# Latents' cross attention: context normalised with features over partitions, running maxima put into the score banks by ScalarE

## The reference

```python
def layernorm(t, g, b):
    mu = jnp.mean(t, axis=-1, keepdims=True)
    var = jnp.var(t, axis=-1, keepdims=True)
    return (t - mu) * jax.lax.rsqrt(var + EPS) * g + b
xn = layernorm(x, ln_x_g, ln_x_b)              # x: the context, 512 features
ln = layernorm(latents, ln_l_g, ln_l_b)
q = ln @ Wq                                    # 16 heads of 64
k, v = jnp.split(jnp.concatenate((xn, ln), axis=1) @ Wkv, 2, axis=-1)
sim = jnp.einsum('bhid,bhjd->bhij', q * scale, k)
sim = jnp.where(mask_full[:, None, None, :], sim, max_neg)
out = jnp.einsum('bhij,bhjd->bhid', softmax(sim), v)
return layernorm(out.transpose(0, 2, 1, 3).reshape(b, m, INNER) @ Wout, ln_o_g, ln_o_b)
```

## Time and profile before

| what | value |
|---|---|
| median of 3 runs | 2112.92 us (2111.11 to 2114.09) |
| the profiled execution's own time | 2115.48 us |
| its span, first to last instruction | 2113.3 us |
| mean granted clock of PE | 0.970 |
| busy: PE, DVE, ACT, POOL | 94%, 74%, 49%, 31% of the span |
| the pipeline of `context_attention_1` | about 820 to 1852 us |
| span of one body in it | 59.5 us |

### The profile page before, as it was taken

The page is one execution under the profiler, slowest core; times in us unless marked ns, Lnnn a source line. Parts: engine busy times, 40 slices in busy tenths (PEclk is TensorE's granted clock), DMA queues, the critical chain, the costliest instruction groups (busy, mean ns, idle before and its releaser), DMA issues. The chain is left out here.

```text
span 2113.3 us, 45029 instructions
## 1 busy us (share of the span) xinstructions
PE 1977.3 (94%) x18290; PEld 1103.7 (52%) x18290; DVE 1569.6 (74%) x2777; ACT 1044.0 (49%) x1484; POOL 657.6 (31%) x696
## 2 busy tenths in 40 slices
PE   7899999999789788999999999999999999888998
PEld 3455555555555443455555555555555555544643
DVE  4689999999857673677777777777777776654676
ACT  2689998998813542333333333333333333323453
POOL 3244444454412230133333322333333322313100
PEclk9899999999799899999999999999999999999999
DMA  4323323322133210000000000000000000210300
GB/s 149 103 54 99 93 65 95 97 64 72 31 142 116 108 41 22 22 23 23 23 4 20 23 23 23 23 23 23 23 2 23 23 23 2 81 46 0 145 21 20
DMA packets 39613, 106.22 MB, mean 50 GB/s; under 512 B 19312, under 2 KB 21616, under 8 KB 33264
## 3 DMA queue, kind: packets, MB, share of 16 engines
q1 hardware_dynamic: 39408, 103.35, 16.1%
HBM read 75.42 MB, written 1.05 MB: 36 GB/s over the span
## 5 line engine op out<-in xcount | busy, mean ns | idle before, releaser
L1468 POOL TENSOR_SCALAR a1c_p_hi<-a1c_pf 128x512 f16<-128x512 f32 x272 | 201.1, 740 | 666.6 <-ACT a1c_pf L1524 624.1
L1326 PE MATMUL PS<-a_x_hi,w_next 128*128 128x512 f16 x1088 | 280.9, 381 | 3.8 <-DVE a1c_v_lo L1598 1.7
L1336 PE MATMUL PS<-w_next,a_x_hi 128*128 128x512 f16 x1088 | 279.0, 379 | 0.0
L1493 ACT ACTIVATE a1c_k_hi<-PS 128x512 f16<-128x512 f32 x136 | 81.2, 597 | 329.4 <-PE PS L1326 329.4
L375 POOL TENSOR_SCALAR a0c_p_hi<-a0c_r 128x1024 f16<-128x1024 f32 x128 | 154.9, 1210 | 268.7 <-DVE a0c_r L475 265.8
L1500 ACT ACTIVATE a1c_v_hi<-PS 128x512 f16<-128x512 f32 x136 | 81.6, 600 | 258.8 <-PE PS L1336 206.0
L480 DVE TENSOR_TENSOR a0c_p_lo<-a0c_r,a0c_p_hi 128x1024 f16<-128x1024 f32 x128 | 201.8, 1576 | 0.9 <-POOL a0c_p_hi L375 0.9
L1673 DVE TENSOR_TENSOR a1c_p_lo<-a1c_pf,a1c_p_hi 128x512 f16<-128x512 f32 x272 | 197.8, 729 | 6.0 <-POOL a1c_p_hi L1468 6.0
L1524 ACT ACTIVATE a1c_pf<-PS,a_maskc 128x512 f32<-128x512 f32 x256 | 175.1, 686 | 49.0 <-PE PS L1835 39.0
L1616 DVE CUSTOM_DVE_ANT_0 a1c_junk<-PS,a1c_maskr 128x512 bf16<-128x512 f32 x256 | 175.9, 687 | 18.8 <-DVE a1c_ctop L1616 0.5
L475 DVE TENSOR_TENSOR a0c_r<-PS,a0c_r 128x1024 f32<-128x1024 f32 x128 | 155.4, 1214 | 32.8 <-ACT a0c_r L421 32.6
(11 more groups left out here) (368 smaller groups left out, 4606.3 us busy)
## 6 DMA issues: line engine op xcount, KB each, us to landing
a_cf<-in_ctxT SPq DMA_DIRECT2D x16, 1024.0 KB, 5.2
a0c_ks<-a0c_k_hi SPq DMA_DIRECT2D x128, 128.0 KB, 2.3
a1c_cf<-in_ctx SPq DMA_DIRECT2D x16, 1024.0 KB, 4.8
a0c_ks<-a0c_k_lo SPq DMA_DIRECT2D x64, 128.0 KB, 2.3
f_w<-in_w SPq DMA_DIRECT2D x4, 1024.0 KB, 8.2
f_w<-in_w SPq DMA_DIRECT2D x1, 4096.0 KB, 20.2
qw_raw<-in_w_gate SPq DMA_DIRECT2D x1, 2816.0 KB, 10.3
qw_raw<-in_w_up SPq DMA_DIRECT2D x1, 2816.0 KB, 11.2
```

What stands on the lines that cost most here:

```text
L1326: mm = nc.tensor.matmul(out, wk[i][:, k, f * P:(f + 1) * P], (x_hi, x_lo)[j][e][:, k, :], start=(step == 0), stop=(step == 11))
L1336: mm = nc.tensor.matmul(out, (x_hi, x_lo)[j][e][:, k, t * P:(t + 1) * P], wv[i][:, k, group * BANK:(group + 1) * BANK], start=(step == 0), ...
L1468: nc.gpsimd.tensor_scalar(p_hi[:, v % 4, :], pf[:, v % 2, :], 1.0, 0.0, ALU.mult, ALU.add)\
```

## The change

The context is loaded twice, with rows over partitions (`cf`, now for the moments alone) and with features over partitions (`ct`, from an input laid out that way already). The inverse root and the shift of each row are written to a small tensor in device memory and read back as two rows for all partitions (`spread_rows`, tile `rows`). DVE applies them and the norm's scale in two operations (`context_norm`), ACT adds the norm's bias and makes the f16 part (`context_hi`), DVE the rest (`context_lo`). `normalise`, `turn` and `context_f32` go. `MADE` is 11, the number that `TURN` had.

The diagonal matmuls are done once for each piece and group of heads (`spread_tops`, in slot 13 of the body before and slot 5) into two banks of the ring; ACT copies the result to SBUF (`keep_tops`) and from there, ahead of each unit's scores, into its score bank (`base`). `score` waits for that and adds onto it with `start=False`. Piece 0 keeps the matmuls in `score`.

```diff
+            if j >= 1 and v == SPREAD[0]:
+                RING_ORDER += [("tops", j, 0), ("tops", j, 1)]
+            if j >= 2 and v == SPREAD[1]:
+                RING_ORDER += [("tops", j - 1, 2), ("tops", j - 1, 3)]
...
-                            sp.wait_ge(turned, 4 * c)
+                            sp.wait_ge(stats_done, NT * c)
...
+                        if c >= 1:
+                            sp.wait_ge(x_lo_done, KT * c)
+                        sp.dma_start(ct[:].rearrange("p k n -> p (k n)"), d["ctxT"][c]).then_inc(ct_in, 16)
+                    def spread_rows(c):
+                        if c >= NCH:
+                            return
+                        sp.wait_ge(newton, 5 * (c + 1))
+                        sp.dma_start(rows_out[c % 2].rearrange("a (t p) -> p a t", p=P), rn[:], allow_slow_non_contiguous=True)\
+                            .then_inc(rows_kept, 16)
+                        sp.wait_ge(rows_kept, 16 * (c + 1))
+                        if c >= 1:
+                            sp.wait_ge(x_done, KT * c)
+                        sp.dma_start(rows[:].rearrange("p a n -> p (a n)"),
+                                     rows_out[c % 2:c % 2 + 1].rearrange("o a n -> o (a n)").broadcast_to([P, 2 * CH]))\
+                            .then_inc(rows_in, 16)
...
                     tops(0, 0)
+                    spread_rows(0)
...
                         tops(j, 1)
+                        spread_rows(j + 1)
                         tops(j + 1, 0)
...
-                            if j + 1 < NCH and v == 9:
-                                normalise(j + 1)
                             if j + 1 < NCH and v == 11:
                                 mask_row(j + 1)
-                            if j + 1 < NCH and v > TURN:
-                                context_hi(j + 1, v - TURN - 1)
...
+                    def context_hi(c, k):
+                        act.wait_ge(x_done, KT * c + k + 1)
+                        if c >= 1:
+                            act.wait_ge(v_product, 8 * c)
+                        nc.scalar.activation(x_hi[(c + 1) % 2][:, k, :], ct[:, k, :], ACT.Identity,
+                                             bias=bx[:, k:k + 1]).then_inc(x_hi_done, 1)
...
+                    def keep_tops(j, gp):
+                        for side in range(2):
+                            act.wait_ge(spread, 4 * (j - 1) + 2 * gp + side + 1)
+                            nc.scalar.copy(neg[:, gp, side, :], g.PS[:, ring_bank("tops", j, 2 * gp + side), :])\
+                                .then_inc(neg_done, 1)
+                    def base(j, v):
+                        gp, side = group_of(v), side_of(v)
+                        act.wait_ge(neg_done, 4 * (j - 1) + 2 * gp + side + 1)
+                        act.wait_ge(exp_done, UNITS * j + v - 1)
+                        nc.scalar.copy(g.PS[:, S0 + side, :], neg[:, gp, side, :]).then_inc(based, 1)
...
-                    inverse_root(0)
...
+                        if v == 7:
+                            inverse_root(0)
+                        if MADE <= v < MADE + KT:
+                            context_hi(0, v - MADE)
                     for j in range(NJ):
                         for v in range(UNITS):
                             if j + 1 < NJ and v >= 1:
                                 evacuate(j + 1, v - 1)
-                            if j + 1 < NCH and v > TURN:
-                                context_f32(j + 1, v - TURN - 1)
+                            if j + 1 < NJ and v == SPREAD[0]:
+                                keep_tops(j + 1, 0)
+                            if j >= 1 and v == SPREAD[1]:
+                                keep_tops(j, 1)
+                            if j + 1 < NCH and MADE <= v < MADE + KT:
+                                context_hi(j + 1, v - MADE)
                             probability(j, v)
-                            if j + 1 < NCH and v == 8:
+                            if j + 1 < NJ and v >= UNITS - 2:
+                                base(j + 1, v + 2 - UNITS)
+                            elif j >= 1 and v < UNITS - 2:
+                                base(j, v + 2)
+                            if j + 1 < NCH and v == 6:
                                 inverse_root(j + 1)
                             if j >= 1 and v == 5:
                                 shrink(j)
...
+                    def context_norm(c, k):
+                        if k == 0:
+                            dve.wait_ge(ct_in, 16 * (c + 1))
+                            dve.wait_ge(rows_in, 16 * (c + 1))
+                        nc.vector.scalar_tensor_tensor(out=ct[:, k, :], in0=ct[:, k, :], scalar=gx[:, k:k + 1],
+                                                       in1=rows[:, 0, :], op0=ALU.mult, op1=ALU.mult)\
+                            .then_inc(x_scaled, 1)
+                        dve.wait_ge(x_scaled, KT * c + k + 1)
+                        nc.vector.scalar_tensor_tensor(out=ct[:, k, :], in0=rows[:, 1, :], scalar=gx[:, k:k + 1],
+                                                       in1=ct[:, k, :], op0=ALU.mult, op1=ALU.add).then_inc(x_done, 1)
 
                     def context_lo(c, k):
                         dve.wait_ge(x_hi_done, KT * c + k + 1)
                         e = (c + 1) % 2
-                        nc.vector.tensor_tensor(x_lo[e][:, k, :], xf[:, k % 2, :], x_hi[e][:, k, :], ALU.subtract)\
+                        nc.vector.scalar_tensor_tensor(out=x_lo[e][:, k, :], in0=ct[:, k, :], scalar=bx[:, k:k + 1],
+                                                       in1=x_hi[e][:, k, :], op0=ALU.add, op1=ALU.subtract)\
                             .then_inc(x_lo_done, 1)
+                    def context_step(c, v):
+                        if MADE <= v < MADE + KT:
+                            context_norm(c, v - MADE)
+                        if MADE < v <= MADE + KT:
+                            context_lo(c, v - MADE - 1)
 
...
+                        if 3 <= v < 3 + NT:
+                            moments(0, v - 3)
+                        if v == 8:
+                            newton_step(0)
...
+                        context_step(0, v)
...
-                            if j + 1 < NCH and v in (1, 3, 5, 7):
-                                moments(j + 1, (1, 3, 5, 7).index(v))
-                            if j + 1 < NCH and v == 8:
+                            if j + 1 < NCH and v in (1, 2, 4, 5):
+                                moments(j + 1, (1, 2, 4, 5).index(v))
+                            if j + 1 < NCH and v == 6:
                                 newton_step(j + 1)
-                            if j + 1 < NCH and v > TURN:
-                                context_lo(j + 1, v - TURN - 1)
+                            if j + 1 < NCH:
+                                context_step(j + 1, v)
...
+                    def spread_tops(j, gp):
+                        pe.wait_ge(diag_done, diags_by(j, gp))
+                        for side in range(2):
+                            r = half(side)
+                            freed("tops", j, 2 * gp + side)
+                            nc.tensor.matmul(g.PS[:, ring_bank("tops", j, 2 * gp + side), :], negones[r, :],
+                                             diag[j % 2][r, 4 * gp:4 * gp + 4, :, :].rearrange("p f a n -> p (f a n)"),
+                                             start=True, stop=True).then_inc(spread, 1)
...
-                        if j >= 1 or v >= 2:
-                            pe.wait_ge(exp_done, UNITS * j + v)
...
+                        else:
+                            pe.wait_ge(based, UNITS * (j - 1) + v + 2)
...
+                            if j + 1 < NJ and v == SPREAD[0]:
+                                spread_tops(j + 1, 0)
+                            if j >= 1 and v == SPREAD[1]:
+                                spread_tops(j, 1)
```

More of the change, by code:

```diff
@@ L1210, in context_attention_1 @@
                 RING_ORDER.append(("plain", j if v else j - 1, v - 1 if v else H - 1))
+            if j >= 1 and v == SPREAD[0]:
+                RING_ORDER += [("tops", j, 0), ("tops", j, 1)]
+            if j >= 2 and v == SPREAD[1]:
+                RING_ORDER += [("tops", j - 1, 2), ("tops", j - 1, 3)]
             RING_ORDER.append(("values", j, v // 2) if v % 2 else ("keys", j, v // 2))
-            if TURN <= v < TURN + KT and j < NCH:
-                RING_ORDER.append(("turn", j, v - TURN))
-    RING_ORDER += [("plain", NCH, H - 2), ("plain", NCH, H - 1)]
+    RING_ORDER += [("plain", NCH, H - 2), ("plain", NCH, H - 1), ("tops", NCH, 2), ("tops", NCH, 3)]
     PLACE = {use: n for n, use in enumerate(RING_ORDER)}
@@ L1378, in context_attention_1 @@
                 "stats_done", "aggr_done", "var_done", "ln_done", "y0_done"))
-            newton, z_done, turned, x_done, x_hi_done, x_lo_done = (s.sem(n) for n in (
-                "newton", "z_done", "turned", "x_done", "x_hi_done", "x_lo_done"))
```

(32 more changed lines are left out.)

50 lines of the change are left out of this document (15 added, 35 removed).

## The result

The changed kernel takes **2254.55 us** (median, 2250.45 to 2258.28) against 2113.51 in the same session: ratio 1.065, interval 1.061 to 1.069. Forecast: 2239. Its profiled run took 2256.0 us, 140.5 more than that of before.

A forecast was written before the change was run, and what follows sets the result against it. PE's instruction stream was taken to bound the kernel. Waits 113, clock 15, start -4, body 15 -1, last body +3 sum to +126 on 2115.5, 2241; the median, 2.6 lower, gives 2239 us, range 2185 to 2300.

The forecast's parts named there:

- The ring: Slots 11 to 14: DVE's norm and ACT's in-order queue take turns, 27.7 us from 1091.75 to the next body's first score.
- Loop: Bodies 0 to 14: each 7.5 us slower from waits less the shorter stream, plus 1 us of clock loss.
- the clock's own part: PE's clock falls around its waits: 1 us a body, 15 us in all, ends 0 and 3.4 a body.
- PE's waiting time: PE waits some 10.3 us in each of 15 bodies, in three places: before scores 12, 14 and 0.
- two of the signs: PE busy 60 to 70% in slots 11 to 15; first `score` matmul waiting three times a body, some 150 us.
- The range's rival: The clock stays low in and after the waits, 3.4 us of work a body: 2275, or 2300; 15%.
- PE's stream: Bodies 0 to 14: transposes 1.76 and diagonals 1.8 leave, spreads add 0.8; 2.8 us shorter each, 42 in all.
- The prices: Operation times assumed for ACT and DVE: `base` 0.60 us, norm operation 0.69, `context_hi` 0.50 to the next start.
- The first norm: DVE's slot 11: first `context_norm` done at +5.05 us, counted from 1091.75.
- The prologue: Start: a 2.6 us wait, half clock and transposes go, late norms and rows give back 3; together -4, -8 to +5.
- The rows in the loop: `spread_rows` through memory: in 7 to 16 us after newton, 16 us of cover before the first norm, no cost taken.
- The end: Last body, without projections: `base` stands between exp and score where PE rests already; +3 us.

The follow-up runs named there:

- e1: Changed kernel with ACT's `context_hi` moved behind `base`, one slot later (slots 12 to 15): 2124.0 us, ratio 1.0037.
- e4: Changed kernel without the second operation of `context_norm` (the mean is not subtracted): 2200.14 us, ratio 1.041.
- e6: Changed kernel with 44 matmuls whose result nobody reads ahead of PE's wait for `base` in slots 12 and 14: 2244.8 us, ratio 1.062.
- e13: e7 with DVE's norms and `context_lo` and ACT's `context_hi` laid around the crowded slot 12: 2093.31 us, ratio 0.987.
- e5: e1 with the prologue's moments and Newton steps two slots earlier and the rows' write and read ahead of the tops' copies on SP: 2112.92 us, ratio 0.999.
- e3: Kernel before with only the maxima's half of the change (`spread_tops`, `keep_tops`, `base`), transposes kept: 2114.41 us, ratio 1.000.
- e2: Only the context's half of the change, diagonals back in the scores, no `base`, `keep_tops` or `spread_tops`: 2219.45 us, ratio 1.048.
- e11: Only the context's half of the change in e7's order, diagonals in the scores, no `base`, `keep_tops` or spread: 2109.2 us, ratio 0.998.
- e7: e5 with `moments` in slots 0 to 3, Newton in slot 5, norms from slot 10, one slot earlier: 2105.64 us, ratio 0.996.
- e8: e5 with rows multiplied and added by GpSimd, DVE applying scale and bias in one operation, moments and Newton as in e7: 2117.93 us, ratio 1.002.

## Why the prediction was right, and where it was not

The measured time, 2254.55 us, is 15.5 above the forecast and within its range, and the mechanism is the one forecast.

- **The ring: right.** Its place, its order and its 60 waits in the loop came as told. Counted as in the forecast, from where PE goes over to the output behind product 10, one pass takes 28.2 us where 27.7 was worked out (1051.67 to the end of `base` for the next body's second score at 1079.84). e1 shows that it is the cause, and e4 that DVE's time in it counts one for one.
- **Loop: right in sum.** Forecast 7.5 + 1 a body, measured 8.7. With the clock held up (e6) a body is 67.5 against 67.0 forecast, and the clock's own part is 0.7 against 1. The ring was 0.5 us longer than worked out and the clock cost 0.3 less, and these two errors nearly cancel.
- **PE's waiting time: too large.** It came out smaller than 10.3 us: about 7.4 idle a body, in two visible waits of some 3.5 us each. The third, before score 0, hides behind PE's slow work. For this reason two of the signs failed: from 1051 to 1080 us PE is busy for 75% and not 60 to 70%, and the wait at `score` comes two and not three times a body, 122 us and not 150. The range's rival (3.4 us a body of lost clock on top) had the lost work nearly right: 68.2 less 7.4 idle and less a stream of 56.85 leaves 4.0. It missed that this work fills the wait.
- **PE's stream**: 2.8 us shorter forecast, 2.65 by the spacing of the rows (8 x 0.22 + 1.76 - 2 x 0.43). The shortest body reached shows less: e13's 58.0 with 0.6 of waiting is 2.1 below 59.5.
- **The prices**: `base` 0.589 us against 0.60; each norm operation 0.75 against 0.69; `context_hi` 0.722 and 0.62 to the next start, against 0.50. Over four turns the last two make the ring some 1 us longer. The first norm came at +4.5 and not at +5.05, which took back half of it. The Trainium skill (ScalarE: Activation LUTs, "Step-by-step: what each stage is for") has PSUM as the faster destination; this trace does not show a gain: `base`, SBUF to PSUM, takes 0.589 and `keep_tops`, PSUM to SBUF, 0.590. The two read from different memories as well, so they do not single out the destination.
- **The prologue: wrong.** "Together -4" was +3.4. The step that failed is that late norms and rows give back some 3 us: DVE waited 10.3 us for the rows, with PE behind it (10.6). PE then had a granted clock of 0.50 up to 870 us, and its next product took 5.06 us instead of 2.6. e5, with the rows asked for earlier, gives 11 us back.
- **The rows in the loop: right, barely.** On SP the write is issued at 1106.56, the read at 1117.86:

```profile
1106.56 0.38 SPq L1419 DMA_DIRECT2D a1c_rows_out<-a1c_rn  x1
1117.86 0.33 SPq L1424 DMA_DIRECT2D a1c_rows<-a1c_rows_out  x1
```

  With 4.2 us of reading they are in at 1122.1, and the first norm starts at 1123.3. The trip is 15.5 us, close to the upper bound (16), and 16.8 us of cover hid it. The Trainium skill (DMA: Bandwidth & Descriptors, "Rules for kernel authors") has one descriptor for each element of such a stride. The page of the profile agrees: packets under 512 B went from 19312 to 36464, which is 1072 more for each of the 16 chunks, and a chunk's rows have 1024 elements.
- **The end: mis-sized.** +3 forecast, +7.8 found behind the last mark. PE's last output is 4.8 us later after that mark (13.0 to 17.8), and the granted clock is 0.67 from 1972 to 1998 us, where the kernel before has 1.00. e3 has the same 17.8, while e2 and e11, which have no `base`, have 13.7: these some 4 us belong to `base` between exp and score. The other 3 lie behind the last output, in work that the change does not touch. They are not `base`'s: there e2 is 4.3 and e11 5.3 us longer than before, with a granted clock of 0.80 around the last output. Their cause is open.

The 15 us between 2239 and 2254.6 are thus the prologue (7.4) and the end (4.8), with 2.7 from the bodies.

## What to carry over

When a step moves to an in-order queue, ask what it waits for and what stands behind it. An engine that is idle a quarter of its time can still set the pace if another engine's queue is stopped by it, and its operations then count one for one. Put the waiting step behind everything that others need, and count the backlog (work that has been released and not yet done) slot by slot: DVE's mean load of 85% in e7 says nothing of its slot 12, with 1.2 + 2.06 + 1.45 + 0.67 = 5.4 us of work in 3.5. A clock loss inside a wait that something else sets is nearly free; fill such waits only if the work behind them is what ends last.

## What the runs showed of the hardware

- Writing 1024 four-byte elements to memory took 11.3 us in the loop (from its issue at 1106.56 to the next at 1117.86); reading them back to 128 partitions, 512 KB, took 4.2 (median).
- In e8 a GpSimd `tensor_tensor` of 128x512 f32 took 1.58 us on average in the loop, and 1.26 at best in the prologue. With it, DVE's operations on SBUF became longer: 0.75 to 0.83 on average for `p_lo`, 0.69 to 1.22 for the diagonals.
- ACT wrote 512 columns of PSUM from bf16 in SBUF in 0.589 us, and 512 columns of bf16 in SBUF from PSUM in 0.590.
